# An octonion feed-forward and attention kernel: the second chunk of the first group computed as gate, up, gate, up

## The reference, cut to what matters

```python
def ternary_dequant(W):
    scale = jnp.mean(jnp.abs(W))
    return scale * jnp.clip(jnp.round(W / scale), -1.0, 1.0)      # value of the original's expression
def oct_ternary_linear(xp, W):                                    # xp: (..., 8, d)
    M = jnp.einsum('jik,jod->koid', S_OCT, ternary_dequant(W))    # octonion product: 8 parts by 8 parts
    return jnp.einsum('...id,koid->...ko', xp, M)
xn = layernorm(x)                                                 # x: (1, 2048, 1024)
gate, up = oct_ternary_linear(xn, w_gate), oct_ternary_linear(xn, w_up)   # 8 x 341 hidden
out = oct_ternary_linear(silu(gate) * up, w_down)
corr = irfft(rfft(xn) * conj(rfft(xn)))                           # autocorrelation of each row
weights, delay = top_k(corr, 6)                                   # softmax of these, a sum of shifted rows
x = x + sum_k softmax(weights)[k] * roll(xn, -delay[k]) + out
```

## Time and profile before

| what | value |
|---|---|
| median of 3 runs | 612.71 us (612.17 to 613.39) |
| the profiled execution | 611.43 us, its span 609.6 us |
| PE busy | 575.1 us, 94% of the span |
| PE weight load busy | 533.8 us, 88% |
| DVE busy | 506.1 us, 83% |
| POOL busy | 463.1 us, 76% |
| ACT busy | 356.4 us, 58% |
| granted TensorE clock, whole span | 0.998 |
| longest waits of PE after its first | 2.8 us, 2.0 us, and six of 0.7 us |

### The profile page before, as it was taken

The page is one execution under the profiler, slowest core; times in us unless marked ns, Lnnn a source line. Parts: engine busy times, 40 slices in busy tenths (PEclk is TensorE's granted clock), DMA queues, the critical chain, the costliest instruction groups (busy, mean ns, idle before and its releaser), DMA issues.

```text
span 609.6 us, 16256 instructions
## 1 busy us (share of the span) xinstructions
PE 575.1 (94%) x6672; PEld 533.8 (88%) x6672; DVE 506.1 (83%) x1227; ACT 356.4 (58%) x499; POOL 463.1 (76%) x362
## 2 busy tenths in 40 slices
PE   0998999989999999999999999999999999999996
PEld 0898998878989999899989998899989998999896
DVE  1875799769899889989898989989888989967854
ACT  4767885755556645865567645774476545543540
POOL 2403919999778986999769977999779977987920
PEclk9999999999999999999999999999999999999999
DMA  9520003001030022101030013002030012002011
GB/s 226 135 72 1 1 1 140 2 1 57 16 139 2 2 72 65 76 2 70 2 140 1 9 65 126 15 2 71 2 139 1 35 38 70 2 2 70 2 71 70
DMA packets 10235, 30.65 MB, mean 50 GB/s; under 512 B 913, under 2 KB 4017, under 8 KB 10161
## 3 DMA queue, kind: packets, MB, share of 16 engines
q1 hardware_dynamic: 9200, 28.22, 13.9%
q10 hardware_dynamic: 960, 1.40, 1.0%
HBM read 21.23 MB, written 8.39 MB: 49 GB/s over the span
## 4 chain that ended last, share of the span: by engine, by line
POOL 53%; issue 30%; PE 12%; DVE 1%; DMA 1%; ACT 1%; POOLq 0%; SPq 0%; ACTq 0%
POOL hop L1299 15%; POOL hs L1293 10%; POOL hs L1294 10%; POOL hs L1289 9%; POOL hs L1288 6%; PE acc L462 5%; PE acc L393 4%; DMA xr<-in_x 1%; PE acc L372 1%; POOL r L1247 1%; POOL hop L1296 1%; PE acc L439 1%; PE acc L404 0%; PE acc L365 0%; ACT junk L584 0%
## 5 line engine op out<-in xcount | busy, mean ns | idle before, releaser
L462 PE MATMUL acc<-wd,hop 114*128 114x128 f16 (+1 forms) x2944 | 169.7, 219 | 1.0 <-POOL hop L1299 0.7
L462 PEld LDWEIGHTS acc<-wd,hop 114*128 114x128 f16 (+1 forms) x2944 | 166.6, 98 | 2.3 <-POOL hop L1299 0.9
L664 ACT ACTIVATE pk<-acc 114x512 f32<-114x512 f32 (+1 forms) x120 | 70.6, 589 | 70.4 <-PE acc L462 34.0
L1288 POOL TENSOR_TENSOR hs<-hx 114x512 f32<-114x512 f32 x47 | 60.3, 1283 | 66.8 <-DVE hx L1058 59.0
L1299 POOL TENSOR_TENSOR hop<-hs,hop 114x1024 f16<-114x1024 f32 x46 | 98.2, 2136 | 7.9 <-ACT hop L719 7.9
L1296 POOL TENSOR_TENSOR hop<-hx,hop 114x1024 f16<-114x1024 f32 x46 | 98.4, 2138 | 0.6 <-ACT hop L708 0.6
L372 PE MATMUL acc<-xop,wg 128*128 128x256 f16 x704 | 84.1, 273 | 4.5 <-DVE acc L1009 4.4
L708 ACT ACTIVATE hop<-hx 114x1024 f16<-114x1024 f32 x46 | 48.6, 1057 | 65.4 <-DVE hx L1058 65.4
L365 PE MATMUL acc<-xop,wg 128*128 128x256 f16 x704 | 84.2, 273 | 1.2 <-DVE hx L1058 1.1
L372 PE MATMUL acc<-xop,wu 128*128 128x256 f16 x704 | 84.1, 273 | 0.7
L365 PE MATMUL acc<-xop,wu 128*128 128x256 f16 x704 | 84.1, 273 | 0.7 <-DVE hx L1058 0.7
(11 more groups left out here) (156 smaller groups left out, 913.3 us busy)
## 6 DMA issues: line engine op xcount, KB each, us to landing
xr<-in_x SPq DMA_DIRECT2D x16, 512.0 KB, 4.6
zx<-in_x SPq DMA_DIRECT2D x16, 512.0 KB, 3.6
out_y<-zx SPq DMA_DIRECT2D x16, 512.0 KB, 3.0
hop<-in_w_down SPq DMA_DIRECT2D x1, 1364.0 KB, 19.1
hop<-in_w_gate ACTq DMA_DIRECT2D x1, 1152.0 KB
hop<-in_w_up SPq DMA_DIRECT2D x1, 1152.0 KB
hop<-in_w_gate ACTq DMA_DIRECT2D x1, 192.0 KB
hop<-in_w_up SPq DMA_DIRECT2D x1, 192.0 KB
```

The lines of the kernel that those rows point to most:

```text
L462: last = nc.tensor.matmul(acc[:, bank[n], s // 2, at:at + P], operand(g, c, t, form, level), wd[0:WIDE[c], slot, c, :], start=which == 0 a ...
L664: nc.scalar.activation(pk[0:rows, q % 2, :, :], pair[:, :, T:2 * T], ACT.Copy, scale=XS if u[0] == "X" else 1.0).then_inc(copied, 1)
L1288: nc.gpsimd.tensor_tensor(hs[:, 4:8:2, :], h[:, 0:4:2, :], h[:, 1:4:2, :], ALU.add)
```

## The change

In `opening`, on TensorE and on ScalarE the second chunk of group 0 goes as G 0 1 0, U 0 1 0, G 0 1 1, U 0 1 1 (it was G, G, U, U), and T 2 1 goes ahead of X 1 1. U 0 1 0 gets bank 3, G 0 1 1 bank 0. On VectorE `ternary` and `weight_slots` of T 0 1 go ahead of `least`, and `weight_slots` of T 2 0 ahead of that of T 1 1. On ScalarE `signs` of T 1 1 goes ahead of the normalisation of group 1, and `h_sums_high` of U 0 1 0 goes out of the loop into the opening, ahead of `eights` of T 0 1. `eights` of T 2 2 goes into the loop.

```diff
@@ opening @@
-               (("X", 1, 0), 3), (("G", 0, 1, 0), 0), (("T", 2, 0), 1), (("X", 1, 1), 2), (("G", 0, 1, 1), 3), (("T", 2, 1), 1),
-               (("U", 0, 1, 0), 0), (("T", 2, 2), 1), (("U", 0, 1, 1), 2))
+               (("X", 1, 0), 3), (("G", 0, 1, 0), 0), (("T", 2, 0), 1), (("T", 2, 1), 1), (("X", 1, 1), 2), (("U", 0, 1, 0), 3),
+               (("T", 2, 2), 1), (("G", 0, 1, 1), 0), (("U", 0, 1, 1), 2))
@@ tables of the loop @@
-    round_at = {OPEN + 1: ("U", 0, 1, 0), OPEN + 4: ("U", 0, 1, 1)}
+    round_at = {OPEN + 4: ("U", 0, 1, 1)}
@@ tensor @@
             direct(("G", 0, 1, 0), 1)
+            weights(("T", 2, 1))
             x_unit(("X", 1, 1))
+            direct(("U", 0, 1, 0), 0)
+            direct(("U", 0, 1, 0), 1)
             direct(("G", 0, 1, 1), 0)
-            weights(("T", 2, 1))
+            weights(("T", 2, 2))
             direct(("G", 0, 1, 1), 1)
-            direct(("U", 0, 1, 0), 0)
-            weights(("T", 2, 2))
-            direct(("U", 0, 1, 0), 1)
             direct(("U", 0, 1, 1), 0)
@@ scalar, eights @@
+                if u == ("T", 2, 2):
+                    act.wait_ge(term_mm, prod_no["G", 0, 1, 1] + 1)
@@ scalar, the list @@
             absolute(2)
+            signs(("T", 1, 1))
             normalise(1, 0)
             normalise(1, 1)
-            signs(("T", 1, 1))
...
-            silu(("G", 0, 1, 1))
...
+            eights(("T", 2, 0))
+            signs(("T", 2, 2))
             eights(("T", 0, 0))
             eights(("T", 1, 0))
-            eights(("T", 2, 0))
-            signs(("T", 2, 2))
+            eights(("T", 2, 1))
+            h_high(("U", 0, 1, 0))
+            silu(("G", 0, 1, 1))
+            h_sums_high(("U", 0, 1, 0))
             eights(("T", 0, 1))
-            eights(("T", 2, 1))
-            eights(("T", 2, 2))
-            h_high(("U", 0, 1, 0))
...
+                if n == OPEN + 2:
+                    eights(("T", 2, 2))
@@ vector, weight_slots @@
                 if u == ("T", 2, 2):
-                    dve.wait_ge(term_mm, prod_no["G", 0, 1, 1] + 1)
+                    dve.wait_ge(term_mm, prod_no["U", 0, 0, 1] + 1)
@@ vector, the list @@
             product(("U", 0, 0, 0))
-            least(("F", 0))
             ternary(("T", 0, 1))
             weight_slots(("T", 0, 1))
+            least(("F", 0))
             ternary(("T", 1, 1))
...
+            weight_slots(("T", 2, 0))
             weight_slots(("T", 1, 1))
-            weight_slots(("T", 2, 0))
             weight_slots(("T", 2, 1))
```

More of the change, by code:

```diff
@@ L102, in octonion_ffn_attention_kernel @@
     x_no, f_no, t_no = rank("X"), rank("F"), rank("T")
-    slots_no = {("T", *t): i for i, t in enumerate(((0, 2), (1, 0), (1, 2), (0, 1), (1, 1), (2, 0), (2, 1), (2, 2)))}
-    eights_no = {("T", *t): i for i, t in enumerate(((0, 2), (1, 2), (0, 0), (1, 0), (2, 0), (0, 1), (2, 1), (2, 2), (1, 1)))}
+    slots_no = {("T", *t): i for i, t in enumerate(((0, 2), (1, 0), (1, 2), (0, 1), (2, 0), (1, 1), (2, 1), (2, 2)))}
+    eights_no = {("T", *t): i for i, t in enumerate(((0, 2), (1, 2), (2, 0), (0, 0), (1, 0), (2, 1), (0, 1), (1, 1), (2, 2)))}
     g_no, u_no, n_no = rank("G"), rank("U"), rank("N")
@@ L757, in _ @@
             x_high(("X", 1, 0))
+            negate(("T", 1, 1))
             h_sums_high(("U", 0, 0, 0))
-            negate(("T", 1, 1))
             signs(("T", 2, 0))
+            h_high(("U", 0, 0, 1))
             x_sums_high(("X", 1, 0))
@@ L764, in _ @@
             x_high(("X", 1, 1))
-            h_high(("U", 0, 0, 1))
+            signs(("T", 2, 1))
+            h_sums_high(("U", 0, 0, 1))
             eights(("T", 0, 2))
-            h_sums_high(("U", 0, 0, 1))
-            signs(("T", 2, 1))
             x_sums_high(("X", 1, 1))
             eights(("T", 1, 2))
-            silu(("G", 0, 1, 1))
+            eights(("T", 2, 0))
+            signs(("T", 2, 2))
             eights(("T", 0, 0))
             eights(("T", 1, 0))
-            eights(("T", 2, 0))
-            signs(("T", 2, 2))
+            eights(("T", 2, 1))
+            h_high(("U", 0, 1, 0))
+            silu(("G", 0, 1, 1))
+            h_sums_high(("U", 0, 1, 0))
             eights(("T", 0, 1))
-            eights(("T", 2, 1))
-            eights(("T", 2, 2))
-            h_high(("U", 0, 1, 0))
             for n in range(OPEN, N + 8):
```

## The result

The changed kernel takes 614.09 us (median of 20 runs, 611.54 to 616.61), the kernel before 612.2 us in the same comparison (20 runs, 608.95 to 613.39). The ratio is 1.0047, 95% interval 1.003 to 1.0065: slower by about half a percent. The profiled execution has a span of 611.4 us against 609.6.

What follows compares the result with a forecast made beforehand. GpSimd's chain was taken to set the pace from 98.2 to 144.0 us, TensorE afterwards. Late additions of +1.48 and +0.11 us made about +1.6, added to 612.71 for 614.3 us; range 611.4 to 615.8.

Steps and rivals of the forecast that it cites:

- the chain: Passage into the loop: VectorE's additions to G 0 2 0 1.48 us late, U 0 2 1's 0.11 more; +1.59 us.
- the copy: ScalarE's copy of G 0 2 0's odd parts, queued behind rounding and eights: starts at 96.47 instead of 94.99.
- GpSimd's late instruction: GpSimd's last instruction of U 0 2 0: moves from 116.64 to 118.23 us.
- The opening: TensorE through with the opening 1.87 us earlier, at 91.1.
- The delay of the normalisation: ScalarE: T 1 1's signs hold the normalisations, X 1 0 waits from 58.16 to about 58.43; TensorE's gain is 1.87 us, not 2.14.
- T 2 1 ahead of X 1 1: TensorE: 0.87 us more of transposes in front of X 1 1, which starts at 68.03 instead of 69.03.
- VectorE's shift of 1.22: VectorE's dense stretch behind X 1 1's rounding, up to the product of U 0 1 0, starts 1.22 us earlier.
- The eights of T 2 2 in the loop: ScalarE, behind silu of G 0 2 0: U 0 2 1's odd parts ready at 105.17, wanted at 105.06; +0.11 us.
- Gate, up, gate, up: VectorE: the same 16.39 us stand before U 0 1 0's product, so it starts at 87.10, not ten microseconds earlier.
- GpSimd's rival: Passage into the loop: GpSimd's chain decides and ScalarE is in time; 1.2 us faster, 611.5 us; chance 0.13.
- The clock rival: TensorE's clock falls in the pause ahead of G 0 2 0's terms; 1.75 us more, 616.1 us; chance 0.07.
- cases still longer: A VectorE wait in its dense stretch, beyond the forecast's slowdown; 0.05 within the chance of slower.

Runs made afterwards that it cites:

- the last experiment: Changed kernel with the rounding of U 0 1 0 back in the loop, X 1 1 ahead of T 2 1, normalisation ahead of T 1 1's signs: 608.88 us, ratio 0.9953.
- the filled pause: Changed kernel with 28 matmuls that nobody reads in TensorE's 3.5 us pause ahead of G 0 2 0's terms: 612.99 us, ratio 1.0027.

## Why the prediction was right, and what it left out

*The direction and the size of the chain.* +1.59 was forecast, +1.64 and +1.65 measured in the stretch, by the way that was described: the copy starts at 95.96, which is 96.55 on before's clock (forecast 96.47), GpSimd's late instruction at 118.29 (forecast 118.23). The kernel with the rounding back in the loop shows the cause by taking it out.

*The small terms.* The opening was 1.80 us shorter (51.47 to 49.67) against 1.87; X 1 0 waited 0.20 and not 0.27. The delay of the normalisation and T 2 1 ahead of X 1 1 each turned out to cost 0.39 us of the stretch, measured one by one: 0.78 together, where I had 0.27 and 0.65, the 0.92 us by which VectorE's shift of 1.22 falls short of TensorE's possible 2.14. The eights of T 2 2 in the loop cost about what was forecast: VectorE's first addition of U 0 2 1 comes 0.1 us late.

*Gate, up, gate, up.* I said that the product is not brought forward, as 16.4 us of VectorE's work stand in front of it. It is so (16.39 us again, from 70.19 to 86.58 in the changed kernel), and by the last experiment the order is then worth nothing that one profile of each kernel can show.

*GpSimd's rival.* Its price was right too: with the copy free the stretch is 1.31 us below before's, where the rival had 1.2. The point at which I had it turn, the product of U 0 1 0 before 84.4, stays untested, as the run with the early product lost more on VectorE than it freed on ScalarE.

*What was mis-sized is the clock.* I gave the fall of TensorE's clock 0.07 and a price of 1.75 us. In runs of the changed kernel it is the rule: 24 of 32 have the lower mean clock, average 615.0 us against 612.1 of the other 8, and the filled pause takes 1.6 us from the median. The 1.75 us fit the sixteen matmuls (1.48 to 1.66 us more in three profiles with a fall there), but not the 2.8 us between the two sets of runs. Neither of the changed kernel's own two profiles has a fall in the new pause, so that it happens there rests on the kernels with the eights behind and with the minimum first, which keep the pause, and on the filled one. The argument against it, that a pause of 2.76 us had not made the clock fall, rested on one execution. The changed kernel's own profile has a fall just there, after a pause of 2.75 us (columns of the earlier trace rows):

```profile
139.00:141.00 2.00, 1.92 (x10) 1.86 (x11) 1.73 (x7) 1.94 (x3) 2.00 (x2) 0.50 0.00 0
```

One execution shows that something can stay away, not that it does. Of all twelve profiles only before's has none at X 2 0 or within 2 us of it. So this fall is no mark of the change; it also stands in versions that are faster than before.

The difference is thus about 2.9 us by the ratio (0.47% of 612.2), 1.65 of it the chain, and 1.9 us between the two medians, as the runs of both kernels lie at several levels. That 614.3 us came so close to 614.09 is in part luck: the chain was added to a median of three runs, 612.71, where the kernel before has 612.2 over twenty, and that half microsecond stands in for clock time that I had left out. The clock rival's single number, 616.1, is too high for a median, though the slowest runs (616.61) are there. The chances had a slip too: the five add up to 1.00, and the 0.05 for cases still longer was taken from the rivals without a word.

## What to carry to other kernels

When a step is moved on an engine with an ordered list, price it by what is queued behind it while it waits. A rounding whose source is another engine's late result belongs behind the copies that are ready. A saved wait is worth what it moves in the chain that ends last, and moving one line for it was worth more here than the rebuilt order. Ahead of a plan to start an engine earlier, look at which operations of its neighbour will then run beside it.

## What the runs showed of the hardware

*VectorE and GpSimd slow each other in some operations.* Beside a working GpSimd, VectorE's float16 additions with both inputs in SBUF took 1.6 us each instead of 0.36 (6.46 against 1.43 for four), and were back at 0.36 when GpSimd was held. Its float32 additions with an input in PSUM kept 0.42 us beside the same kind of GpSimd work (sums of 114x512) in the loop. It is not the number format: a row dot, whose two inputs are float32 in SBUF, takes 0.69 us alone and 1.56 beside GpSimd. The Trainium skill, "GPSIMD Engine Reference", section 8, says that GpSimd shares its SBUF interfaces with VectorE and that they contend where a VectorE instruction has two SBUF inputs. The runs agree and give the price. I could have read it from the profile before. This is VectorE's second row dot in it:

```profile
90.31 1.56 DVE L920 SCALAR_TENSOR_TENSOR dj<-xr 128x512 f16<-128x512 f32 x1
```

The one ahead of it, which had begun before GpSimd did, took 0.69 us. GpSimd's first two sums of U 0 1 0, at 89.67 and 91.28, took 1.65 and 1.71 us, and the next two 1.27 and 1.26 (the first and the last are in the earlier trace rows). The opening kept the slots ahead of GpSimd's work and so out of this.

*TensorE's clock fell to its lower level, 1.2 GHz, after pauses of 2.3 to 5.9 us,* in some executions and not in others. Behind a pause ahead of G 0 2 0's terms sixteen matmuls took 3.39 us after 2.34 us, 3.48 after 3.47 and 3.57 after 5.94, but 1.91 after 3.47 in both profiles of the changed kernel. Ahead of X 2 0, behind about 2.75 us, the granted clock was 0.50 in the changed kernel and 1.00 in the profile before. The mean clock of a run counts these falls: 0.998 in the profile with none, 0.996 or 0.997 in those with the one at X 2 0, 0.993 or 0.991 in those with one more at G 0 2 0's terms. What decides whether it falls in a given run stays open here.

*Runs with the same mean clock still differ by up to 2 us.* U 0 0 0 starts at 39.1 to 39.8 us in five of the twelve profiles and at 40.8 to 41.5 in the other seven. The two profiled runs of the changed kernel, both at 0.996, differ by 1.91 us (613.26 and 611.35) and their starts by 1.81 (40.92 and 39.11), so the difference arises ahead of the stretch. What makes the start early or late I have not tested.
